# Two steps' weighted sums in one visit, and evacuations one step behind, in a cross-attention kernel

## The reference

```python
x = x + attention(layernorm(x), ctx, ctx, mask)      # q,k,v = rows @ W.T; softmax(clip(q.k / sqrt(32), -50, 50)); @ Wo.T
x = x + int8_ffn(layernorm(x), rhs)                  # rows quantised to int8 by their absmax, dot with quantised rhs, rescaled
```

## Time and profile before

| what | value |
|---|---|
| median of the runs | 2001.1 us |
| profiled execution, device time | 1992.74 us |
| its span | 1990.6 us |
| PE busy | 1838.3 us (92%) |
| DVE busy | 1530.5 us (77%) |
| ACT busy | 1294.5 us (65%) |
| GpSimd busy | 254.9 us (13%) |
| mean granted TensorE clock | 0.97 |

### The profile page before, as it was taken

How to read it: one execution, slowest core, us unless ns; L and a number is a source line. 1 busy time by engine, 2 the same in 40 slices (tenths; PEclk the granted TensorE clock), 3 DMA queues, 4 the chain that set the end, 5 groups by cost and what they waited for, 6 DMA issues and landing times.

```text
span 1990.6 us, 36936 instructions
## 1 busy us (share of the span) xinstructions
PE 1838.3 (92%) x10584; PEld 1006.6 (51%) x10584; DVE 1530.5 (77%) x1857; ACT 1294.5 (65%) x1682; POOL 254.9 (13%) x200
## 2 busy tenths in 40 slices
PE   5886999999998999999899999989999999999996
PEld 4775555545454555645455554545655433333333
DVE  4334788878786879878788887878888887877875
ACT  3333777767776676766667666666776776767652
POOL 0000011111010111111111110111121111111113
PEclk9998999999998999999999999999999999999997
DMA  6468264645556364554626556363555544446332
GB/s 214 140 179 212 61 166 123 169 113 138 143 152 156 98 176 111 158 154 131 179 74 171 145 144 171 111 172 94 150 156 141 146 112 123 128 102 154 74 112 96
DMA packets 224962, 276.23 MB, mean 139 GB/s; under 512 B 27520, under 2 KB 142208, under 8 KB 224128
## 3 DMA queue, kind: packets, MB, share of 16 engines
q1 hardware_dynamic: 224768, 274.28, 51.3%
HBM read 181.41 MB, written 92.54 MB: 138 GB/s over the span
## 4 chain that ended last, share of the span: by engine, by line
PE 63%; issue 17%; DVE 6%; DMA 5%; ACT 5%; POOL 1%; SPq 1%; DVEq 1%; ACTq 0%; POOLq 0%
PE tile L723 21%; PE scores L761 20%; PE wsum L774 18%; ACT probs L934 3%; DVE acc L1164 3%; DMA den_c<-denoms 2%; PE dsum L786 1%; PE tile L854 1%; DMA denoms<-recip_row 1%; DMA k_parts<-stage_hi 1%; DMA row_lo<-o_parts 1%; PE tile L830 1%; POOL normed L1226 1%; PE dsum L780 0%; SPq L538 0%
## 5 line engine op out<-in xcount | busy, mean ns | idle before, releaser
L934 ACT ACTIVATE probs<-scores 128x1024 f32<-128x1024 f32 x1024 | 993.9, 1024 | 451.7 <-PE scores L761 408.3
L1164 DVE TENSOR_TENSOR acc<-acc,probs 128x1024 f32<-128x1024 f32 x864 | 1083.8, 1292 | 120.1 <-ACT probs L934 109.3
L761 PE MATMUL scores<-q_stack,k_stack 128*128 128x512 f32 x2048 | 642.4, 431 | 22.3 <-ACT probs L934 17.2
L761 PEld LDWEIGHTS scores<-q_stack,k_stack 128*128 128x128 f32 x2048 | 343.2, 191 | 533.9 <-ACT probs L934 400.1
L774 PE MATMUL wsum<-probs,v_sb 128*32 128x512 f32 x4096 | 556.4, 615 | 22.4 <-DVEq L1151 21.2
L1164 DVE TENSOR_TENSOR acc<-probs 128x1024 f32<-128x1024 f32 x64 | 76.6, 1222 | 145.4 <-PE dsum L786 91.5
L774 PEld LDWEIGHTS wsum<-probs,v_sb 128*32 128x32 f32 x4096 | 82.2, 109 | 175.4 <-issue 113.0
L1218 POOL TENSOR_TENSOR rstd<-var_eps,minus_half 128x1 f32<-128x1 f32 x56 | 33.6, 600 | 906.7 <-DVE var_eps L1060 906.7
L723 PE MATMUL tile<-ctx_hi,wk_hi 128*128 128x256 f32 x448 | 129.4, 289 | 21.4 <-DVE wk_lo L1014 17.9
L723 PE MATMUL tile<-ctx_hi,wk_lo 128*128 128x256 f32 x448 | 128.2, 286 | 0.0
L723 PE MATMUL tile<-ctx_lo,wk_hi 128*128 128x256 f32 x448 | 127.5, 285 | 0.0
(11 more groups left out here) (153 smaller groups left out, 1799.0 us busy)
## 6 DMA issues: line engine op xcount, KB each, us to landing
k_stack<-k_parts SPq DMA_DIRECT2D x256, 256.0 KB, 5.7
q_stack<-q_parts SPq DMA_DIRECT2D x128, 256.0 KB, 6.7
v_parts<-v_stage SPq DMA_DIRECT2D x64, 256.0 KB, 2.4
v_sb<-v_parts SPq DMA_DIRECT2D x64, 256.0 KB, 5.4
raw<-ctxT SPq DMA_DIRECT2D x28, 512.0 KB, 5.5
k_parts<-stage_hi SPq DMA_DIRECT2D x96, 128.0 KB, 2.9
k_parts<-stage_lo SPq DMA_DIRECT2D x96, 128.0 KB, 2.4
k_parts<-q_stack SPq DMA_DIRECT2D x64, 128.0 KB, 3.4
```

Source lines behind the costliest of these rows:

```text
L761: last = nc.tensor.matmul(scores[:, h, :], k_stack[:, kt // 4, h, (kt % 4) * P:(kt % 4 + 1) * P], q_stack[:, qb, h, :], start=True, stop=True)
L934: nc.scalar.activation(probs[:, slot % RING, 2 * pair:2 * pair + 2, :], scores[:, 2 * pair:2 * pair + 2, :], ACT.Exp, scale=1.0 / math.sqr ...
L1164: nc.vector.tensor_tensor(acc[:, heads, :], other, now, ALU.add).then_inc(sems["add_done"], 1)
```

## The change

PE now makes weighted sums in odd slots alone: in slot s those of steps s-3 and s-2, one behind the other. ACT handles the pieces of slot s-1 in slot s, behind the two exponentials of slot s. DVE handles the K, Q, X and N pieces of slot s-1 in slot s, behind the first add of slot s; X was until now done at the start of the next slot. The store DMAs of pieces, the copies of `dsum` and `wsum` and the chain behind them go one slot later, and so does the load of the next output rows.

```diff
-    27: [("next_orows",), ("T", 1), ("V", 1, 1, 0)], 28: [("V", 1, 1, 1)], 29: [("V", 1, 1, 2), ("flag",)],
+    27: [("T", 1), ("V", 1, 1, 0)], 28: [("next_orows",), ("V", 1, 1, 1)], 29: [("V", 1, 1, 2), ("flag",)],
-SOON = "KQN"
+SOON = "KQXN"
# SyncE
-                        if slot == first + 2:
+                        if slot == first + 3:
                             ct.wait_alone(sp, "denoms_copied", k)
...
-                    for p in seg.pieces(slot):
+                    for p in seg.pieces(slot - 1 if seg.b else slot):
# TensorE
-                    if summing:
-                        for pair in range(2):
-                            sums_of(slot - LAG, pair)
+                    if summing and slot % 2 == 1:
+                        for step in (slot - LAG - 1, slot - LAG):
+                            for pair in range(2):
+                                sums_of(step, pair)
# ScalarE
-                    for p in seg.at(slot):
+                    late = seg.b
+                    for p in seg.at(slot) if not late else [q for q in seg.at(slot) if q[0] not in PIECES] + seg.pieces(slot - 1):
-                        if on and slot == first + 1:
+                        if on and slot == first + 2:
                             ct.wait(act, "acc_summed", k)
# VectorE
-                                for p in seg.at(slot):
+                                for p in seg.at(slot - 1):
                                     if p[0] in SOON:
                                         row_work(p)
-                        if on and slot == first + 4:
+                        if on and slot == first + 5:
```

More of the change, by code:

```diff
@@ L638, in iteration @@
                             load_residuals(sp, ct, 1)
-                        if slot == first + 5:
+                        if slot == first + 6:
                             ct.wait_alone(sp, "recips_ready", k)
                             sp.dma_start(recip_row.rearrange("h (a j) -> (h a) j", j=G * QB // P), recip_c[:, :]).then_inc(sems["recips_stored"], 16)
-                        if slot == first + 6:
+                        if slot == first + 7:
                             ct.wait_alone(sp, "recips_stored", 16 * k)
@@ L645, in iteration @@
                                 .then_inc(sems["recips_loaded"], 16)
-                        if slot == first + 10:
+                        if slot == first + 11:
                             ct.wait_alone(sp, "attn_split", k)
@@ L913, in between @@
                     nc.scalar.copy(rhs_scale[:, :], scores[:, 0, :]).then_inc(scale_copied, 1)
+                    act.wait_ge(w_done, 4)
                     return
@@ L1227, in body @@
                     for first, k, on in ((0, 0, seg.prev), (KT, 1, seg.b)):
-                        if on and slot == first + 8 and (seg.b or seg.c):
+                        if on and slot == first + 9 and (seg.b or seg.c):
                             normalise(ct, k)
```

## The result

The changed kernel takes 2300.3 us (median of 4 runs, 2295.46 to 2301.86) against 2001.4 us, ratio 1.1485 (95% interval 1.1463 to 1.1508): slower by 299 us. The forecast was 2265 us in a range of 2165 to 2375.

The account below looks back on a forecast made before the run. PE was taken to bound nearly all slots of iterations with stage A. The profiled 1992.7 us plus 219 net from the slot terms plus 45 for the clock made 2257, forecast as a median of 2265 us, range 2165 to 2375.

Parts of the forecast that it names:

- PE bounds the filled slots: Nearly all slots in the 12 iterations with stage A: a microsecond PE saves or loses is one of the program.
- The visit, 0.30 us: Each sum visit of PE left out saves 0.30 us, in 256 places 77 us, if nothing else happens.
- Even slots without cover: Next scores wait for exponentials: 0.5 us with a V or O third, 1.4 without a piece, none with K or Q.
- Late evacuations: PE waits for pieces ACT and DVE evacuate a slot late: 20.3 us an iteration, 15.5 without stage C.
- Slots 7, 20 and 24: N waits for the squares of the K or Q piece before it: 2.75, 2.5 and 2.5 us.
- Slot 18: K(1,2) waits for the low part of K(1,0), X(1) for K(1,1): 0.75 + 1.3 = 2.05 us.
- Slot 13: F waits for the copy of V(0,1), O for the low part of X(0): 1.25 us more.
- Slot 5: K waits for the low part of the piece two back, made by DVE behind an add: 0.25 us.
- The clock, +45: After 76 new waits of 2 us or more, 45 falls of PE's clock at 1.0 us each: +45 us.
- DVE's signal, -12: Ahead of an iteration's first sum, now one slot later: 5 waits, 2.4 us of each covered, -12 us.
- Stores and chain at nothing: Moved stores, copies and chain steps cost nothing, or up to 0.6 us in slots 3 and 19.
- The signs: Iterations with A, B, C about 142 us, without A 95; 36 waits before L854; PE about 80% busy, clock under 0.97.

Follow-up runs that it names:

- the joined visit alone: The kernel before with the sums of two steps joined in odd slots, evacuations and chain where they were: 2023.9 us, ratio 1.011.
- the last experiment: The kernel before with sums joined only in pairs (6,7), (16,17), (20,21), (22,23), (24,25) of iterations with stage A: 1987.8 us, ratio 0.992.

## Why the prediction was right, step by step

- **PE bounds the filled slots: right.** Each group of waits taken away came back in time, 273 us in all of the 276 between the changed kernel and the joined visit alone.
- **The visit, 0.30 us: nearly.** The five pairs with a long even piece that the last experiment joins gave 0.17 to 0.34. Taken over all 256 places it does not pay, since the waits of the scores grew from 17.2 to 76.9 us.
- **Even slots without cover: right in kind, a little small.** A pair without pieces took 5.43 us (forecast 5.3), a pair of thirds 6.36 where 0.5 - 0.3 on 6.13 gave 6.33. I had balanced visit and exponentials at -5 us with the DVE signal's 12; the visit alone measured +22. The iterations of B and C came out as forecast (20). The mis-sized places are pair (12,13), where I gave the full saving and 8.5 us were lost, and pair (4,5), whose wait for O I did not have.
- **Late evacuations: right, with one term too small.** Slots 7, 20 and 24: 88.7 us measured, 2.75 + 2.5 + 2.5 in 12 iterations forecast, 93. Slot 19: 30.5 us against 32. Slot 21: 29.0 against 31. Slots 10 and 27: 27.4 in 16 waits, against 28. Slot 18: 17.4 (both of its waits) against 25. Slot 13: F alone waited 23.9 us (8 times), and only 1.0 us of waits for `row_lo` was left behind it; I had put the longer wait at O. Slot 5 is the term that was too small: 0.25 in 12 iterations, 3 us, against 12.9 us in 10 waits, up to 2.7 us each.
- **The clock, +45: a little small.** 72 low stretches against 23 before are 49 more, where I had counted 45 falls; their 161 us are 60 us at the rate of the filler experiment, 1.2 a fall where I took 1.0. That waits of over 2 us bring the clock down is what the filler experiment shows: filled, they did so no more.
- **DVE's signal, -12: the direction is shown.** It went from 21.2 to 3.3 us. The three traces here whose first sum stands in slot 2 show 18.1 to 27.2 us, the seven with it in slot 3 show 3.3 to 11.3. The size differs from trace to trace.
- **Stores and chain at nothing: right in the changed kernel** (2.2 us of waits for the copy of `wsum`), but only as the sums moved along with it; alone it cost 32.6 us.
- **The signs.** Iterations with A, B and C went from 118.0 to 143.1 us (forecast 142), those without A from 90.4 to 95.8 (95); PE's busy share is 83% (80), the clock 0.939, and N waited 36 times.

The medians missed by 35 us: 15 are the clock's. Of the rest, pair (4,5) is the largest place: over the 12 iterations with stage A it grew by 23 us in the profiled executions, where the sum had next to nothing, with the waits of slot 5 and 5.5 us of waits for O in slot 4 in it. Errors the other way, as in slot 18, made the total look better than its parts.

## What to carry to other kernels

Before evacuations are put behind the next step's work, list for each of them who awaits it and in which step: those awaited in the very next step stall the producer for the whole of what was put ahead, and those awaited two steps on can stall it too, as K(0,0) did in slot 5 (15.5 us over the program). The stores and the copies moved without a cost that could be seen, as long as their readers moved too. Joining visits to save a change of matmul form paid here only where other work stands between the two score blocks for as long as the exponentials take. A part of a change can hide a wait that the other part makes, so both halves have to be tried alone.

## What the hardware showed beyond that

Useless matmuls in a wait made the kernel 35 us faster: with 16 of them ahead of each of 36 waits the mean granted clock rose from 0.939 to 0.959. They are 256-column matmuls on weights that are there anyway, and cost nothing that could be seen in their place, since N started when it did before. The pairs of the filled slots gained 42 us and the program 35, as the clock fell more often elsewhere, so such a filler has to be measured over the whole program.
